# One cross-attention stage on TensorE: values computed once per chunk of keys, in place of context rows summed by the probabilities and projected at the end

## The chip, the cores and the metric

The kernel runs on one NeuronCore of a Trainium2 chip, as one program. Its metric is the time on the device in microseconds. Five engines work side by side, each through its own queue in order: TensorE (PE; its loads of stationary operands are shown as PEld), VectorE (DVE), ScalarE (ACT), GpSimd (POOL) and SyncE (SP), which here issues most of the DMAs. They meet at semaphores alone: every wait in the code is written by hand.

## The reference, cut to what matters

The reference is a small Perceiver block on 128 latent rows of width 256: a cross-attention on a context of 12544 rows (this stage is the one that changes), a banded self-attention, a mixture of experts, a second cross-attention, a scan and a second mixture of experts. The stage in question is

```python
# x1: [1,128,256] (normalised latents), x2: [1,12544,256] (context), 16 heads of 64
q = x1 @ Wq
kv = x2 @ Wkv
k, v = jnp.split(kv, 2, axis=-1)
q, k, v = map(_split_heads, (q, k, v))
attn = jnp.einsum('bhid,bhjd->bhij', q, k) * SCALE
attn = jax.nn.softmax(attn, axis=-1)
out = jnp.einsum('bhij,bhjd->bhid', attn, v)
b, h, l, d = out.shape
out = out.transpose(0, 2, 1, 3).reshape(b, l, h * d)
return out @ Wo + bo
```

All arithmetic is to be that of fp32. The kernel gets there with TensorE's rounded fp32 (F32R): an operand is split into a high part, rounded, and a low part, the rest, and three products (high by high, high by low, low by high) are added in PSUM.

## The kernel before

The stage is `stage_context`. The context is cut into 14 chunks of 896 keys (`CK`; `NT` = 7 tiles of 128). The loop goes over 224 steps, one for each chunk and head: `u = 16 * chunk + head`. Softmax is kept as a running one: `nm` holds the negated maximum, `al` the factor by which the old sums shrink, `den` the denominators, `U` the sums.

Keys are explicit. A "piece" `p` (L494) is half a chunk (448 keys) for a pair of heads, six F32R matmuls into one bank of PSUM; ScalarE writes its high parts (L339) and VectorE its low parts (L405) into the tile `K`. Pieces run five steps ahead (`AHEAD`). The values are not explicit: the probabilities multiply the raw context (`cNh`, `cNl`, 256 wide), `U` holds 256 numbers for each latent and head, and the value weight `wv` comes in after the last step.

One step `u` on TensorE: seven transposes of the probabilities (L553) into two banks, piece `u+5`, the scores of step `u+2` (four matmuls, L504 and L505), and the sum over the keys `O` (L579): 21 matmuls of 256 columns, seven each for high by high, high by low, low by high. ScalarE, meanwhile: high part of the transposed probabilities (`pTh`, L368), high parts of the piece (L339), the factor `al` (L344) and the exponentials of step `u+1` (L346). VectorE: maximum of the scores of step `u+1` (L410) and the new `nm` (L415), low part of the transposed probabilities (`pTl`, L449), low parts of the piece (L405), `den` (L460), and `U = U * al + O` (L463).

After the last step come, for eight pairs of heads, four transposes of `U` (L520), a copy by ScalarE (L353), eight matmuls with `wv` (L533), two copies (L429, L430) and two matmuls with `wo` (L599); two of the pairs are partly done in the last steps. GpSimd splits the context twice a chunk, once as it stands (`cNh`, `cNl`) and once transposed (`cTh`, `cTl`).

Order is set by the code: each engine's instructions stand in the order in which its block writes them. The later stages are the same in both kernels.

## Time and profile before

| | us |
|---|---|
| median of 3 runs (1625.44 to 1628.65) | 1627.57 |
| the profiled execution's own time | 1630.0 |
| its span, first to last instruction | 1628.3 |

| engine | busy us | share of the span |
|---|---|---|
| PE (matmul) | 1541.0 | 95% |
| PEld (weight load, beside PE) | 1448.6 | 89% |
| DVE | 1211.6 | 74% |
| ACT | 910.9 | 56% |
| POOL | 364.7 | 22% |

The mean granted clock of TensorE is 0.973 of full. The steps begin at about 36 us and the last one ends near 1225 us, so some three quarters of the span are this loop; the stage's result is ready at 1243.3 us. Shares are means over stages with different limits; the rows of one step say more. In them the first number is the start, the second the duration, a bracket names how long the engine had been idle and for whom it waited. Matmuls overlap: the distance between two starts, not the duration, is what one costs.

### The profile page before, as it was taken

The numbers are of one execution on the slowest core, as the hardware profiler recorded it, in microseconds if no ns is written. First come the engines' busy times: TensorE is split into PE (matmuls) and PEld (weight loads), VectorE is DVE, ScalarE is ACT, GpSimd is POOL, SyncE is SP. The second block draws the span as 40 slices with busy tenths as digits, with TensorE's granted clock in tenths as the row PEclk, the third lists the DMA queues.
The fourth block names the chain that finished last, engine by engine and source line by source line (L and its number), as shares of the span: only waits on it lengthen the run. The fifth ranks groups of instructions, "written<-read, shape, count | busy, mean of one in ns | idle before, by whom it ended". The sixth has DMA issues, their size and how long they took to land. (4 is left out here: it accounts for less than half of the span.)

```text
span 1628.3 us, 26553 instructions
## 1 busy us (share of the span) xinstructions
PE 1541.0 (95%) x10481; PEld 1448.6 (89%) x10481; DVE 1211.6 (74%) x2060; ACT 910.9 (56%) x1616; POOL 364.7 (22%) x166
## 2 busy tenths in 40 slices
PE   5999999999999999999999999999997889999478
PEld 4999999999999999999999999999995778888348
DVE  5878878878878878878878878888874446666764
ACT  4666666666666666666666666666651245555120
POOL 6211111111111111120303030210000236666230
PEclk8999999999999999999999999999998799999779
DMA  4100000000000001010100000100004412111600
GB/s 149 46 23 24 23 24 24 24 23 24 24 24 23 24 4 43 1 46 1 46 2 26 21 24 24 75 2 1 1 1 168 188 46 68 68 68 45 271 1 4
DMA packets 10321, 70.13 MB, mean 43 GB/s; under 512 B 2313, under 2 KB 2912, under 8 KB 8929
## 3 DMA queue, kind: packets, MB, share of 16 engines
q1 hardware_dynamic: 9198, 67.51, 11.2%
q8 instruction: 77, 1.26, 0.3%
q10 hardware_dynamic: 1010, 1.07, 0.2%
q14 instruction: 36, 0.29, 0.1%
HBM read 68.44 MB, written 0.13 MB: 42 GB/s over the span
## 5 line engine op out<-in xcount | busy, mean ns | idle before, releaser
L368 ACT ACTIVATE pTh<-ps 128x896 fp32r<-128x896 f32 x224 | 206.3, 921 | 352.0 <-PE ps L553 352.0
L405 DVE TENSOR_TENSOR K<-ps,K 64x448 fp32r<-64x448 f32 x448 | 278.8, 622 | 67.4 <-ACT K L339 64.2
L339 ACT CAST K<-ps 64x448 fp32r<-64x448 f32 x448 | 236.9, 529 | 78.2 <-PE ps L494 72.3
L449 DVE TENSOR_TENSOR pTl<-ps,pTh 128x896 fp32r<-128x896 f32 x224 | 244.5, 1092 | 4.0 <-ACT pTh L368 4.0
L410 DVE TENSOR_REDUCE nmx<-ps 128x1 f32<-128x896 f32 x224 | 242.8, 1084 | 2.7 <-PE ps L505 2.7
L346 ACT ACTIVATE prob<-ps,nm 128x896 f32<-128x896 f32 x224 | 226.1, 1009 | 2.7
L579 PEld LDWEIGHTS ps<-cNh,pTh 128*128 128x128 f32 x1568 | 218.0, 190 | 10.0 <-issue 3.0
L579 PE MATMUL ps<-cNh,pTh 128*128 128x256 f32 x1568 | 224.0, 283 | 1.8 <-ACT pTh L368 1.7
L579 PE MATMUL ps<-cNh,pTl 128*128 128x256 f32 x1568 | 225.0, 283 | 0.0
L579 PE MATMUL ps<-cNl,pTh 128*128 128x256 f32 x1568 | 224.7, 283 | 0.0
L463 DVE SCALAR_TENSOR_TENSOR U<-U,al,ps 128x256 f32<-128x256 f32 x224 | 107.5, 480 | 146.3 <-PE ps L579 145.6
L553 PE MATMUL ps<-ident,prob 128*128 128x128 f32 x1568 | 207.8, 273 | 1.5 <-ACT prob L346 1.5
L579 PEld LDWEIGHTS ps<-cNh,pTl 128*128 128x128 f32 x1568 | 204.3, 192 | 0.2
L579 PEld LDWEIGHTS ps<-cNl,pTh 128*128 128x128 f32 x1568 | 204.3, 192 | 0.0
L553 PEld LDWEIGHTS ps<-ident,prob 128*128 128x128 f32 x1568 | 176.8, 142 | 2.1 <-issue 2.1
L270 POOL TENSOR_TENSOR cTh<-raw,zero 128x1792 fp32r<-128x1792 f32 x14 | 44.5, 3176 | 566.4 <-PE ps L494 560.0
L504 PE MATMUL ps<-K,qh 128*128 128x448 f32 x448 | 164.8, 368 | 3.3 <-ACT ql L361 3.3
L505 PE MATMUL ps<-K,ql 128*128 128x448 f32 x448 | 164.5, 367 | 0.0
L494 PE MATMUL ps<-cTh,wkh 128*128 128x448 f32 x448 | 146.6, 408 | 1.4 <-DVE wkh L392 1.4
L494 PE MATMUL ps<-cTh,wkl 128*128 128x448 f32 x448 | 127.7, 366 | 5.2 <-DVE wkl L394 5.2
L494 PE MATMUL ps<-cTl,wkh 128*128 128x448 f32 x448 | 128.8, 368 | 0.0
L270 POOL TENSOR_TENSOR cNh<-raw,zero 128x1792 fp32r<-128x1792 f32 x14 | 44.5, 3175 | 279.9 <-PE ps L579 270.9
(298 smaller groups left out, 2027.3 us busy)
## 6 DMA issues: line engine op xcount, KB each, us to landing
raw<-in_ctxT SPq DMA_DIRECT2D x14, 896.0 KB, 4.6
raw<-in_ctxN SPq DMA_DIRECT2D x14, 896.0 KB, 4.5
d_raw<-in_ctxT SPq DMA_DIRECT2D x14, 896.0 KB, 4.5
w<-in_w SPq DMA_DIRECT2D x2, 4096.0 KB, 18.1
wg<-in_wg SPq DMA_DIRECT2D x1, 4352.0 KB, 25.6
wu<-in_wu SPq DMA_DIRECT2D x1, 4352.0 KB, 18.3
wd<-in_wd SPq DMA_DIRECT2D x1, 4352.0 KB, 28.6
e_ea<-in_alog SPq DMA_DIRECT2D x1, 2048.0 KB, 8.4
```

The costliest lines, as they stand in the source:

```text
L339: nc.scalar.copy(K[halves[s], slot, cols], ps[halves[s], piece_bank(p), 0:HK]).then_inc(sem("kh_ready"), 1)
L346: nc.scalar.activation(prob[:, :, :], S[b], ACT.Exp, bias=nm[:, par, h:h + 1], scale=1.0, accum_out=rs[:, b:b + 1]).then_inc(sem("exp_done ...
L368: nc.scalar.activation(pTh[:, :], pT_ps, ACT.Copy).then_inc(sem("pTh_ready"), 1)
L405: ins = nc.vector.tensor_tensor(K[halves[1 - s], slot, cols], ps[halves[s], piece_bank(p), 0:HK], K[halves[s], slot, cols].bitcast(F32), A ...
L410: nc.vector.tensor_reduce(nmx[:, :], S[u % 2], mybir.AxisListType.XY, ALU.max, negate=True).then_inc(sem("chunk_max"), 1)
L449: nc.vector.tensor_tensor(pTl[:, :], pT_ps, pTh[:, :].bitcast(F32), ALU.subtract).then_inc(sem("pTl_ready"), 1)
L463: nc.vector.scalar_tensor_tensor(U[:, h, :], U[:, h, :], al[:, b:b + 1], O, ALU.mult, ALU.add).then_inc(sem("pv_free"), 1)
L494: mm = nc.tensor.matmul(ps[:, piece_bank(p), 0:HK], w[:, k, m * P:(m + 1) * P], x[:, k, half * HK:(half + 1) * HK], start=(n == 0), stop=( ...
L504: nc.tensor.matmul(S[b][:, half, :], qh[:, h, :], keys, start=True, stop=False)
L505: mm = nc.tensor.matmul(S[b][:, half, :], ql[:, h, :], keys, start=False, stop=True)
L553: mm = nc.tensor.transpose(pT_ps[:, k * P:(k + 1) * P], prob[:, :, :].rearrange("p a n -> p (a n)")[:, k * P:(k + 1) * P], ident[:, :])
L579: mm = nc.tensor.matmul(O, w[:, k * P:(k + 1) * P], x[:, k, :], start=(n == 0), stop=(n == 3 * NT - 1))
```

## The change

The values become explicit, for eight heads (a "group", `HG`) and 896 keys at a time. `values(g, i)` computes 128 keys by 8 heads of 64, six F32R matmuls of 512 columns into bank 6. ScalarE writes the high parts of it and VectorE the low parts, side by side for each head, into one of two tiles `V`. It stands in seven of every eight steps (`v_steps`, 189 in the loop; the first group's seven are computed ahead of it). The sum over the keys then has `V` (high and low, 128 columns) as stationary operand and high and low parts of the probabilities (one tile `pT`, 256 columns) as moving one: 7 matmuls in place of 21, with all four products, transposed (`OT_ps`, in the same bank 6 as the values). VectorE adds the two halves into `osb`, an eighth transpose (`turn_sums`) turns that back, and `U` (now 128 wide: high and low value part) is updated one step later. The end loses its products with `wv`.

Also: the context comes in and is split once, transposed; the raw context `cN` goes. `K` has two pairs of slots (`RING` = 2) in place of three. VectorE computes the maximum two steps ahead in place of one. The wide loads of weights come in halves at the start, the value weight among them; the loads that ScalarE's queue issued are SyncE's now. The diff, cut:

```diff
-        O = ps[:, 6, 0:D]
+        turned = ps[:, 4:6, :].rearrange("p b n -> p (b n)")
+        pT_ps = turned[:, 0:CK].rearrange("p (t q) -> p t q", q=P)
+        O_ps = turned[:, CK:CK + P]
+        OT_ps = ps[:, 6, 0:2 * P]
...
             @block.scalar
...
                 def exp_step(u):
+                    act.wait_ge(sem("max_done"), u + 1)
+                    if u >= 4:
+                        act.wait_ge(sem("u_added"), u - 3)
...
                 for u in range(steps):
                     act.wait_ge(sem("p_turned"), u + 1)
-                    nc.scalar.activation(pTh[:, :], pT_ps, ACT.Copy).then_inc(sem("pTh_ready"), 1)
-                    p = u + AHEAD
-                    if p < steps:
...
-                        high_parts(p)
+                    nc.scalar.activation(pT[:, :, 0, :], pT_ps, ACT.Copy).then_inc(sem("pTh_ready"), 1)
                     if u + 1 < steps:
                         exp_step(u + 1)
+                    if u in v_steps:
+                        j = v_steps.index(u)
+                        act.wait_ge(sem("v_done"), NT + j + 1)
...
+                        nc.scalar.copy(v_high(u // HG + 1, u % HG), by_head(ps[:, 6, :])).then_inc(sem("vh_ready"), 1)
+                    if u + AHEAD < steps:
+                        high_parts(u + AHEAD)
...
             @block.vector
...
+                def add_parts(u):
+                    dve.wait_ge(sem("pv_done"), u + 1)
+                    nc.vector.tensor_reduce(osb[:, :], OT_ps.rearrange("p (a q) -> p q a", a=2), AX_X,
+                                            ALU.add).then_inc(sem("o_added"), 1)
+                def update_sums(u):
+                    h, b = u % H0, u % 4
+                    dve.wait_ge(sem("p_turned"), u + 2)
+                    nc.vector.scalar_tensor_tensor(U[:, h, :], U[:, h, :], al[:, b:b + 1], O_ps,
+                                                   ALU.mult, ALU.add).then_inc(sem("u_added"), 1)
...
                 for u in range(steps):
+                    if u >= 1:
+                        add_parts(u - 1)
+                        if u - 1 + AHEAD < steps:
+                            low_parts(u - 1 + AHEAD)
                     dve.wait_ge(sem("pTh_ready"), u + 1)
+                    nc.vector.tensor_tensor(pT[:, :, 1, :], pT_ps, pT[:, :, 0, :].bitcast(F32),
                                             ALU.subtract).then_inc(sem("pTl_ready"), 1)
+                    if u >= 1:
+                        update_sums(u - 1)
...
                     nc.vector.tensor_scalar(den[:, h:h + 1], den[:, h:h + 1], al[:, b:b + 1],
                                             rs[:, b:b + 1], ALU.mult, ALU.add)
+                    if u in v_steps:
+                        j, g, i = v_steps.index(u), u // HG + 1, u % HG
+                        dve.wait_ge(sem("vh_ready"), j + 1)
+                        nc.vector.tensor_tensor(v_low(g, i), by_head(ps[:, 6, :]), v_high(g, i).bitcast(F32),
+                                                ALU.subtract).then_inc(sem("v_split"), 1)
+                    if u + 2 < steps:
+                        max_step(u + 2)
...
             @block.tensor
...
+                def values(g, i, bank):
+                    c, n = g // 2, 0
+                    cols = (left, right)[g % 2]
+                    for x, w in ((cTh[c % 2], wvh), (cTl[c % 2], wvh), (cTh[c % 2], wvl)):
+                        for k in range(KT):
+                            mm = nc.tensor.matmul(ps[:, bank, :], x[:, k, i * P:(i + 1) * P], w[:, k, cols],
+                                                  start=(n == 0), stop=(n == 3 * KT - 1))
+                            n += 1
+                    mm.then_inc(sem("v_done"), 1)
+                def turn_sums(u):
+                    pe.wait_ge(sem("o_added"), u + 1)
+                    return nc.tensor.transpose(O_ps, osb[:, :], ident[:, :])
...
                 for u in range(steps):
                     pe.wait_ge(sem("exp_done"), u + 1)
...
+                    if u >= 1:
+                        mm = turn_sums(u - 1)
                     mm.then_inc(sem("p_turned"), 1)
-                    p = u + AHEAD
...
                         scores(u + 2)
+                    if u in v_steps:
...
+                        values(gn, i, 6)
+                    p = u + AHEAD
+                    if p < steps:
...
+                        piece(p)
...
+                    pe.wait_ge(sem("pTl_ready"), u + 1)
+                    if u in v_steps:
+                        pe.wait_ge(sem("v_split"), v_steps.index(u) + 1)
...
+                    for k in range(NT):
+                        mm = nc.tensor.matmul(OT_ps, V[g % 2][:, k, h % HG, :],
+                                              pT[:, k, :, :].rearrange("p a q -> p (a q)"),
+                                              start=(k == 0), stop=(k == NT - 1))
                     mm.then_inc(sem("pv_done"), 1)
```

How the order moves is best seen engine by engine. TensorE, one step in the middle of the loop, before (`cN` is the context, `ident` the transposes' identity):

```order
L494 MATMUL ps<-cTh,wkh 128x448 x2
L494 MATMUL ps<-cTh,wkl 128x448 x2
L494 MATMUL ps<-cTl,wkh 128x448 x2
L504 MATMUL ps<-K,qh 128x448
L505 MATMUL ps<-K,ql 128x448
L504 MATMUL ps<-K,qh 128x448
L505 MATMUL ps<-K,ql 128x448
L579 MATMUL ps<-cNh,pTh 128x256 x7
L579 MATMUL ps<-cNl,pTh 128x256 x7
L579 MATMUL ps<-cNh,pTl 128x256 x7
L553 MATMUL ps<-ident,prob 128x128 x7
```

and of the change, from the eighth transpose (L550; the seven before it are L594) to the sum over the keys (L635), lines numbered as in the changed kernel:

```order
L550 MATMUL ps<-ident,osb 128x128
L544 MATMUL ps<-K,qh 128x448
L545 MATMUL ps<-K,ql 128x448
L544 MATMUL ps<-K,qh 128x448
L545 MATMUL ps<-K,ql 128x448
L535 MATMUL ps<-wvh,cTh 128x512 x2
L535 MATMUL ps<-wvh,cTl 128x512 x2
L535 MATMUL ps<-wvl,cTh 128x512 x2
L524 MATMUL ps<-cTh,wkh 128x448 x2
L524 MATMUL ps<-cTh,wkl 128x448 x2
L524 MATMUL ps<-cTl,wkh 128x448 x2
L635 MATMUL ps<-pT,V 128x256 x7
```

The scores stand ahead of the piece now, the values between them, and 14 of the 21 wide matmuls are gone. VectorE over the same step, before:

```order
L410 TENSOR_REDUCE nmx<-ps 128x1
L415 TENSOR_SCALAR nm<-nmx,nm 128x1
L449 TENSOR_TENSOR pTl<-ps,pTh 128x896
L405 TENSOR_TENSOR K<-ps,K 64x448 x2
L460 TENSOR_SCALAR den<-den,al,rs 128x1
L463 SCALAR_TENSOR_TENSOR U<-U,al,ps 128x256
```

and of the change (`osb` is the sum of the halves, `V` the low parts of the values):

```order
L438 TENSOR_REDUCE osb<-ps 128x128
L422 TENSOR_TENSOR K<-ps,K 64x448 x2
L480 TENSOR_TENSOR pT<-ps,pT 128x7x128
L444 SCALAR_TENSOR_TENSOR U<-U,al,ps 128x128
L486 TENSOR_SCALAR den<-den,al,rs 128x1
L491 TENSOR_TENSOR V<-ps,V 128x8x64
L430 TENSOR_REDUCE nmx<-ps 128x1
L433 TENSOR_SCALAR nm<-nmx,nm 128x1
```

The maximum has moved from the head of the step to its end, behind the low parts of the values and ahead of the next sum of halves. ScalarE, one step and the head of the next, in the change (before, the casts of `K` stood right behind the copy of the transposed probabilities, and there was no `V`):

```order
L381 ACTIVATE pT<-ps 128x7x128
L361 ACTIVATE al<-nm 128x1
L363 ACTIVATE prob,rs<-ps,nm 128x896
L392 CAST V<-ps 128x8x64
L353 CAST K<-ps 64x448 x2
L381 ACTIVATE pT<-ps 128x7x128
```

The high parts of the values come behind the exponentials of the next step.

## Rows read from the trace of the kernel before

**Rows 1.** Busy time by window: PE, PEld, DVE, ACT, POOL, clock, DMA, GB/s
```profile
60.00:1220.00 1160.00, 1158.32 (x8294) 1124.24 (x8293) 937.37 (x1545) 733.92 (x1306) 173.69 (x48) 1.00 0.06 21
1215.00:1226.00 11.00, 9.09 (x72) 8.21 (x72) 6.81 (x16) 3.71 (x6) 0.00 (x0) 1.00 0.00 0
1243.00:1262.00 19.00, 12.94 (x38) 8.68 (x38) 11.45 (x29) 0.41 (x2) 1.80 (x2) 0.73 0.89 359
```

**Rows 2.** Timeline of one step, weight loads: start us, us, engine, line
```profile
605.51 0.30 PEld L494 LDWEIGHTS ps<-cTh,wkh 128*128 128x128 f32 x2
...
606.63 0.19 PEld L504 LDWEIGHTS ps<-K,qh 128*128 128x128 f32 x1
...
607.44 0.99 PEld L579 LDWEIGHTS ps<-cNh,pTh 128*128 128x128 f32 x7
...
610.06 0.79 PEld L553 LDWEIGHTS ps<-ident,prob 128*128 128x128 f32 x7
```

**Rows 3.** The same step, ScalarE
```profile
605.82 0.92 ACT L368 ACTIVATE pTh<-ps 128x896 fp32r<-128x896 f32 x1 [1.58 <-PE ps L553]
607.03 1.08 ACT L339 CAST K<-ps 64x448 fp32r<-64x448 f32 x2 [0.30 <-PE ps L494]
608.14 0.29 ACT L344 ACTIVATE al<-nm 128x1 f32<-128x1 f32 x1
608.45 1.01 ACT L346 ACTIVATE prob<-ps,nm 128x896 f32<-128x896 f32 x1
609.36 0.19 ACT L346 ACTIVATION_READ_ACCUMULATOR prob<-ps,nm 128x1 f32 x1
```

**Rows 4.** The same step, VectorE
```profile
605.45 1.08 DVE L410 TENSOR_REDUCE nmx<-ps 128x1 f32<-128x896 f32 x1
606.57 0.21 DVE L415 TENSOR_SCALAR nm<-nmx,nm 128x1 f32<-128x1 f32 x1
606.77 1.09 DVE L449 TENSOR_TENSOR pTl<-ps,pTh 128x896 fp32r<-128x896 f32 x1
608.15 1.26 DVE L405 TENSOR_TENSOR K<-ps,K 64x448 fp32r<-64x448 f32 x2 [0.29 <-ACT K L339]
609.44 0.27 DVE L460 TENSOR_SCALAR den<-den,al,rs 128x1 f32<-128x1 f32 x1
610.36 0.48 DVE L463 SCALAR_TENSOR_TENSOR U<-U,al,ps 128x256 f32<-128x256 f32 x1 [0.65 <-PE ps L579]
```

**Rows 5.** The same step, the last two matmuls of the piece
```profile
606.43 0.57 PE L494 MATMUL ps<-cTl,wkh 128*128 128x448 f32 x2
```

**Rows 6.** Groups by form, 512-wide casts and subtractions of the later cross-attention
```profile
L1160 DVE TENSOR_TENSOR d_kNl<-ps,d_kNh 128x512 fp32r<-128x512 f32 x42 | 27.4, 681 | 1.1 <-ACT d_kNh L1095 1.1
L1095 ACT CAST d_kNh<-ps 128x512 fp32r<-128x512 f32 x42 | 23.5, 597 | 28.4 <-PE ps L1238 28.4
```

**Rows 7.** Timeline near the loop's end, where TensorE waits for VectorE
```profile
1217.64 0.21 DVE L415 TENSOR_SCALAR nm<-nmx,nm 128x1 f32<-128x1 f32 x1
1217.77 1.08 DVE L449 TENSOR_TENSOR pTl<-ps,pTh 128x896 fp32r<-128x896 f32 x1
...
1218.91 0.90 PEld L579 LDWEIGHTS ps<-cNh,pTl 128*128 128x128 f32 x7
...
1220.05 0.48 DVE L463 SCALAR_TENSOR_TENSOR U<-U,al,ps 128x256 f32<-128x256 f32 x1 [1.01 <-PE ps L579]
```

**Rows 8.** Timeline around the first step, a matmul at the low clock and the first copy
```profile
32.37 0.57 PE L504 MATMUL ps<-K,qh 128*128 128x448 f32 x1
...
37.27 0.92 ACT L368 ACTIVATE pTh<-ps 128x896 fp32r<-128x896 f32 x1 [1.14 <-PE ps L553]
```

**Rows 9.** Timeline of the stage's end: last copy of probabilities, last projection, result
```profile
1221.25 0.92 ACT L368 ACTIVATE pTh<-ps 128x896 fp32r<-128x896 f32 x1 [0.18 <-PE ps L553]
...
1242.17 0.70 PE L599 MATMUL ps<-wo,oT 128*128 128x256 f32 x2 [0.67 <-DVE oT L430]
1242.91 0.42 DVE L472 TENSOR_TENSOR res<-res,ps 128x256 f32<-128x256 f32 x1 [0.79 <-PE ps L599]
```

More of the change, by code:

```diff
@@ L468, in _ @@
+                    if u + 2 < steps:
+                        max_step(u + 2)
+                    m = (u - (steps - H0)) // 2 - 1
+                    if u > steps - H0 and u % 2 == 0:
+                        scale_sums(m)
+                add_parts(steps - 1)
+                update_sums(steps - 1)
                 scale_sums(PAIRS - 1)
-                for m in range(EARLY, PAIRS):
-                    outputs(m)
                 dve.wait_ge(sem("y0_done"), 1)
@@ new lines, in turn_heads, with project @@
+                def turn_heads(pairs, bank):
+                    pe.wait_ge(sem("U_scaled"), pairs[-1] + 1)
+                    for i, m in enumerate(pairs):
+                        mm = nc.tensor.transpose(ps[:, bank, i * P:(i + 1) * P], U[:, 2 * m, :], ident[:, :])
+                    mm.then_inc(sem("heads_turned"), 1)
+                def project(pairs):
+                    for m in pairs:
+                        mm = nc.tensor.matmul(ps[:, 0, 0:D], oT[:, m, :], wo[:, m, :], start=False,
+                                              stop=(m == PAIRS - 1))
+                    return mm
@@ new lines, in _ @@
+                pe.wait_ge(sem("cT_split"), 1)
+                pe.wait_ge(sem("wk_split"), 1)
+                piece(0)
+                piece(1)
+                piece(2)
+                piece(3)
+                pe.wait_ge(sem("kl_ready"), 1)
+                piece(4)
+                pe.wait_ge(sem("wv_split"), 1)
+                for i in range(NT):
+                    if i == 2:
+                        pe.wait_ge(sem("ql_doubled"), 2)
+                        pe.wait_ge(sem("kl_ready"), 2)
+                        scores(0)
+                        scores(1)
+                    if i < 3:
+                        pe.wait_ge(sem("kl_ready"), i + 2)
+                    else:
+                        pe.wait_ge(sem("first_vl"), i - 1)
+                    values(0, i, first_bank(i))
@@ L604, in stage_mix1 @@
+                project((7,)).then_inc(sem("y0_done"), 1)
 def stage_mix1(nc, t, sb, sem, link, ps, norms, v):
@@ L1701, in layout @@
         "x": a["x"][0],
-        "ctxN": ctx.reshape(n, NT, P, D).transpose(0, 2, 1, 3),
         "ctxT": ctx.reshape(n, CK, KT, P).transpose(0, 3, 2, 1),
```

397 lines of the change are left out of this document (176 added, 221 removed).

## The prediction

> **What bounds the kernel now.** I read the table of windows first. Over the loop [rows 1] the matmuls are busy 1158.3 of 1160 us at the full granted clock, VectorE 81% and ScalarE 63%. A share alone proves nothing, so I went on to the timeline of one step. TensorE's weight loads follow each other without a gap [rows 2]: piece from 605.51 to 606.63 (1.12 us for six matmuls), scores to 607.44 (0.81 for four, 0.20 each), the 21 matmuls of the sum to 610.06 (2.62, 0.125 each), transposes 0.76 (0.11 each). That is 5.31 us, the whole step. ScalarE and VectorE wait for it: 1.58 us ahead of the copy of the probabilities [rows 3], 0.65 us ahead of the update of U [rows 4]. So TensorE's own load is the bound, and taking work from it pays only until some chain of waits takes over.
>
> **TensorE's load after.** A step with values: eight transposes 0.87, scores 0.81, six matmuls of 512 columns 1.37 (0.20 x 512/448 = 0.229 each, an estimate) [rows 2], piece 1.12, sum over the keys 7 x 0.125 = 0.87; together 5.04 us. A step without them: 3.67. Over 189 and 34 steps (the 223 between the first copy and the last) that is 1077 us, where now 1184.0 lie between these copies [rows 8, 9]: 107 us less.
>
> **VectorE's and ScalarE's load after.** VectorE keeps low parts of the piece 1.26, pTl 1.09, den 0.27, maximum 1.08 and nm 0.21 [rows 4]; the update of U falls from 0.48 to about 0.35, as 128 elements fewer at the rate between the 256 of that row and the 896 of pTl, which is 0.95 ns each. It gains the low parts of the values, 0.68 [rows 6], and the sum of halves. For that no row stands: it reads 256 elements from PSUM, and from the maximum's 1.08 for 896 at the same rate it is 0.48 at most and not below 0.40. I take 0.42. By the Trainium skill, "VectorE: DVE Perf Modes", section on the TRN2 errata, a PSUM source costs 120 cycles and one per element at 0.96 GHz, which would be an estimate of 0.39 and 7 us less in all; the rows here run dearer than that rule, 1.08 us for 896 elements where it gives 1.06. The sum on VectorE is 5.4 us, about 4.9 when the 0.08 by which an instruction starts ahead of the end of the one before (1217.77 against 1217.85) [rows 7] is taken off six times. ScalarE: 0.92, 1.41, 0.60 and 1.08, about 4.1. No engine's load reaches the old 5.31 us. The chain does.
>
> **The ring.** Three waits close it: TensorE may not sum over the keys in step u until VectorE has split this same step's values (both live in bank 6); ScalarE takes those values only behind the exponentials; and the copy of the next probabilities waits for the eighth transpose, that is for VectorE's sum of halves, ahead of which VectorE now runs the maximum. I walk it from the start of ScalarE's copy in step u, with 0.03 for a hand-over from ScalarE (606.74 to 606.77) [rows 3, 4] and 0.06 from VectorE to TensorE (1218.85 to 1218.91) [rows 7].
> - Copy 0.92, then al, exponentials and accumulator: 608.14 to 609.55 is 1.41 [rows 3]. ScalarE is free at 2.36.
> - Are the values there? The eighth transpose's load is at -0.42 (it is 0.42 ahead of the copy: the copy starts 0.31 after the next load of TensorE, and one transpose is 0.11) [rows 2, 3]. Scores end at 0.50, the last load of the values is 5 x 0.229 later, and the result is readable 0.60 after the last load (606.43 to 607.03) [rows 3, 5] plus 0.03 for the wider matmul: 2.28. So ScalarE's order decides, by only 0.1 us.
> - High parts of the values: 2.39 to 2.99, 0.60 [rows 6]. Low parts: 3.02 to 3.70.
> - TensorE starts the sum at 3.76; VectorE could read it 1.14 later (1218.91 to 1220.05) [rows 7], at 4.90. VectorE, meanwhile, runs maximum and nm: start 3.62, nm 1.12 later (605.45 to 606.57) [rows 4], next start 0.13 later [rows 7], 4.87. The two are level.
> - Sum of halves 4.88 to 5.30, eighth transpose's load at 5.36, next copy 0.42 later: **5.78 us** for a step with values.
>
> TensorE idles 0.7 us of it, from the end of the piece's loads (0.50 + 1.37 + 1.12 = 2.99) to 3.76. The low parts of keys fit between the sum of halves and the arrival of the high parts of probabilities (they would end at 0.74, pTl starts at 0.95). The high parts of keys run on ScalarE from 3.0 to 4.1 behind the values, with 1.7 us to spare; that cover hides them.
>
> A step without values: copy 0.92, pTl 0.95 to 2.04, sum over the keys from 2.10, readable at 3.24. VectorE has by then update of U, den and the maximum to do (from 1.96: 0.27, 0.20, 1.12, 0.13), free at 3.68; sum of halves to 4.09, load at 4.15, next copy 4.57.
>
> **The sum.** Loop: 189 x 5.78 + 34 x 4.57 = 1092.4 + 155.4 = 1247.8 us, against 1184.0: +63.8. That TensorE does 107 us less and the loop still takes longer is the whole point: the new order buys load with latency.
>
> The end: now 22.1 us from the last copy to the result (1221.25 to 1243.33) [rows 9]. After: copy and pTl 2.04, sum over keys readable at 3.24, halves 3.66, turned 4.14, U 4.49, scaling (three small instructions, about 0.25 each) 5.2, one transpose 5.65, one copy of about 0.4 6.05, projection readable 0.74 later [rows 9] 6.8, addition 0.42: 7.2. That is 14.9 us less; the other pairs lie under the last steps, where TensorE has room.
>
> The start: the first copy is at 37.27 now [rows 8]. Seven blocks of values (9.6 us of TensorE, 4.8 of VectorE) come in ahead of step 0, the first of them under keys' evacuation, and VectorE's long split of the key weight is cut in halves. A walk of it came out within 2 us of the present; I take 0, with -6 to +10 as bounds. The input DMAs are not near any limit in the loop (6% busy) [rows 1], one of the two context transfers goes and GpSimd does half its splits: nothing there waits or is waited for. The later stages are the same: 0.
>
> Sum: +63.8 - 14.9 = +49 us. On the profiled execution's span that is 1677, with the 1.7 around it 1679; on the median 1627.57 it is 1676.5. I forecast **1676 us**.
>
> **Rivals.**
> 1. TensorE's load stays the bound (faster). The ring would have to be shorter than its 5.04 us, for instance since hand-overs, the accumulator's readout or the maximum cost less in it than I add. Time: 1628 - 107 - 15 = 1506. The point from which the sign turns is a value step of 5.78 - 49/189 = 5.52; between it and 5.04 the time lies between. For it: three of my links are level within 0.1 us, so none has hidden slack that adds. Against it: eleven links from rows would have to be 0.26 too long together, and they repeat here within 0.01 from step to step. Chance 0.12, most of it just under 1628.
> 2. TensorE's clock falls (slower). It now pauses some 0.7 us in each value step. At the low level a matmul of 448 columns takes 0.57 in place of 0.37 [rows 8], so 0.20 more for each of four scores, 0.23 for each of six values, 0.1 for each of seven in the sum: about 3 us more in a step. If the clock is low in a tenth of the loop, that is +60: 1736. Against it: between 1215 and 1226 matmuls were busy 9.09 of 11 us, with pauses of a microsecond, at clock 1.00; it fell to 0.73 only where they were busy 12.9 of 19 us [rows 1]. After the change they are busy about seven eighths. Chance 0.07. By the Trainium skill, "TensorE: Matmul & The Clock Gate", section on psum-queue depth-cycling, small idles between groups of matmuls through PSUM can make the clock oscillate; by that rule rival 2 would be the rule and not the exception, and the window of 1215 to 1226 disagrees with it.
> 3. A strided read of PSUM costs twice (slower). The sum of halves steps 128 elements between its two addends. At 0.69 in place of 0.42 it is on the ring every step: 223 x 0.27 = +60, 1737. No row has that pattern. Chance 0.06.
>
> **How the numbers follow.** The forecast holds 0.72: its own range is a ring of 5.6 to 5.95 us (+-34), halves 0.40 to 0.48 (-4 to +13), start -6 to +10, in all 1636 to 1722. A tie with before, 1624 to 1631, gets 0.03 (0.2% either way is what a measurement here can tell from no change). Faster is rival 1, 0.12; slower the rest, 0.85. The range for 8 in 10: 1632 to 1728.
>
> **What would show it.** In the profile after: value steps of 5.8 us and every eighth of 4.6; ScalarE going from the accumulator's readout to the cast of V with almost no wait; TensorE waiting for V of VectorE ahead of the sum over the keys, 0.6 to 0.8 us, 189 times; the maximum ending within 0.1 us of the sum over the keys; granted clock 1.00 in the loop; the stage's end about 7 us after the last copy. I am wrong if TensorE's loads run without a gap (rival 1), if the clock in the loop is below 0.97 (rival 2), if the sum of halves takes over 0.5 us (rival 3), or if ScalarE idles ahead of the cast of V by more than 0.2 us, since then the values come late and the ring goes through TensorE.

## The result and the profile after

The change makes the kernel slower: the median is 1656.68 us (4 runs, 1656.43 to 1657.95) against 1628.11 us (4 runs) for the kernel before on the same chip. The ratio is 1.0175, with a 95% interval of 1.0152 to 1.0197. The forecast was 1676 us in a range of 1632 to 1728, with a chance of 0.85 for slower. The direction is as forecast, clear of the noise but under 2%; of the 49 us forecast, 28.6 came.

| | before | after | |
|---|---|---|---|
| span, us | 1628.3 | 1654.7 | +26.4 |
| start of the first copy of probabilities | 37.27 | 41.49 | +4.2 |
| from the first to the last of these copies | 1184.0 | 1221.5 | +37.5 |
| from the last copy to the stage's result | 22.1 | 9.5 | -12.6 |
| the later stages | 385.0 | 382.2 | -2.8 |

(The rows of before for the first three lines are those of [rows 8, 9].) First the page's line of busy times in the profile after, then its windows (length, then PE, PEld, DVE, ACT, POOL, clock, DMA, GB/s), the first over the loop as [rows 1] was, the second at the stage's end.

```profile
PE 1510.1 (91%) x8657; PEld 1285.2 (78%) x8657; DVE 1368.0 (83%) x2467; ACT 970.2 (59%) x1807; POOL 247.3 (15%) x141
```

```profile
60.00:1240.00 1180.00, 1122.75 (x6490) 959.39 (x6489) 1074.89 (x1919) 784.53 (x1477) 68.93 (x24) 1.00 0.03 10
1262.00:1272.00 10.00, 9.40 (x35) 6.55 (x33) 2.95 (x8) 1.66 (x3) 0.00 (x0) 0.73 0.00 0
```

TensorE's loads fell from 97% of the loop to 81%, and VectorE's share rose from 81% to 91%: no engine is full any more, at a granted clock of 1.00 throughout. That is what a ring looks like in shares. The timeline of one value step of the profile after, TensorE's loads (start us, us, engine, line), without the piece and most of the scores and values:

```profile
602.04 0.14 PEld L550 LDWEIGHTS ps<-ident,osb 128*128 128x128 f32 x1
602.13 0.19 PEld L544 LDWEIGHTS ps<-K,qh 128*128 128x128 f32 x1
602.24 0.19 PEld L545 LDWEIGHTS ps<-K,ql 128*128 128x128 f32 x1
...
606.09 0.89 PEld L635 LDWEIGHTS ps<-pT,V 128*128 128x128 f32 x7 [0.62 <-issue]
...
607.69 0.14 PEld L550 LDWEIGHTS ps<-ident,osb 128*128 128x128 f32 x1
```

ScalarE and VectorE in the same step:

```profile
602.44 0.92 ACT L381 ACTIVATE pT<-ps 128x896 fp32r<-128x896 f32 x1 [1.12 <-PE ps L550]
603.25 0.28 ACT L361 ACTIVATE al<-nm 128x1 f32<-128x1 f32 x1
603.44 1.00 ACT L363 ACTIVATE prob<-ps,nm 128x896 f32<-128x896 f32 x1
604.33 0.19 ACT L363 ACTIVATION_READ_ACCUMULATOR prob<-ps,nm 128x1 f32 x1
604.66 0.59 ACT L392 CAST V<-ps 128x512 fp32r<-128x512 f32 x1
...
608.09 0.92 ACT L381 ACTIVATE pT<-ps 128x896 fp32r<-128x896 f32 x1 [1.12 <-PE ps L550]
...
605.28 0.69 DVE L491 TENSOR_TENSOR V<-ps,V 128x512 fp32r<-128x512 f32 x1 [0.35 <-ACT V L392]
605.88 1.08 DVE L430 TENSOR_REDUCE nmx<-ps 128x1 f32<-128x896 f32 x1
607.00 0.21 DVE L433 TENSOR_SCALAR nm<-nmx,nm 128x1 f32<-128x1 f32 x1
607.21 0.42 DVE L438 TENSOR_REDUCE osb<-ps 128x128 f32<-128x256 f32 x1
```

Read around the ring (the closed chain of waits that the prediction walked), from one load of the eighth transpose to the next: 602.04 to the cast of V at 604.66 is 2.62; to the low parts at 605.28, 0.62; to the load of the sum over the keys at 606.09, 0.81; to the sum of halves at 607.21, 1.12; to the next load at 607.69, 0.48. That is 5.65 us. Steps without values take 4.48. (These are the most frequent distances. In the last chunk every second step is longer, 6.12 and 5.07, of which more below.) The waits of the whole execution (engine, line, for whom: us in all, times, longest) show the same ring from outside:

```profile
ACT pT L381 <- PE ps L550: 253.5, 223, 3.0
PEld ps L635 <- issue: 115.4, 189, 0.6
DVE V L491 <- ACT V L392: 65.7, 189, 0.7
```

Three waits come once in every value step (the first in the others too): for the eighth transpose 1.1 us, for V 0.35 us, and TensorE's 0.6 us ahead of the sum over the keys, 189 times.

### The profile page after: what moved, and what is told of

Same layout as the page of the kernel before. It is cut to its first block and busy times, and to the rows that moved or that the text cites. A ratio compares the mean times of both kernels' runs of the same rounds, so it can differ in the third digit from the quotient of the medians.

```text
span 1654.7 us, 23818 instructions
## 1 busy us (share of the span) xinstructions
PE 1510.1 (91%) x8657; PEld 1285.2 (78%) x8657; DVE 1368.0 (83%) x2467; ACT 970.2 (59%) x1807; POOL 247.3 (15%) x141
## 5 line engine op out<-in xcount | busy, mean ns | idle before, releaser
L381 ACT ACTIVATE pT<-ps 128x896 fp32r<-128x896 f32 x224 | 206.1, 920 | 253.6 <-PE ps L550 253.5
L635 PEld LDWEIGHTS ps<-pT,V 128*128 128x128 f32 x1568 | 199.5, 188 | 125.6 <-issue 115.4
L635 PE MATMUL ps<-pT,V 128*128 128x256 f32 x1568 | 236.4, 290 | 54.9 <-DVE V L491 42.9
L480 DVE TENSOR_TENSOR pT<-ps,pT 128x896 fp32r<-128x896 f32 x224 | 244.5, 1092 | 30.4 <-ACT pT L381 6.8
L594 PE MATMUL ps<-ident,prob 128*128 128x128 f32 x1568 | 208.2, 273 | 0.0
L491 DVE TENSOR_TENSOR V<-ps,V 128x512 fp32r<-128x512 f32 x189 | 130.7, 691 | 65.7 <-ACT V L392 65.7
L594 PEld LDWEIGHTS ps<-ident,prob 128*128 128x128 f32 x1568 | 177.2, 141 | 0.1
L535 PE MATMUL ps<-wvh,cTh 128*128 128x512 f32 x392 | 123.6, 397 | 4.0 <-DVE V L468 4.0
L392 ACT CAST V<-ps 128x512 fp32r<-128x512 f32 x189 | 110.9, 587 | 23.4 <-PE ps L535 0.2
L535 PE MATMUL ps<-wvl,cTh 128*128 128x512 f32 x392 | 123.3, 396 | 0.0
L535 PE MATMUL ps<-wvh,cTl 128*128 128x512 f32 x392 | 122.7, 394 | 0.0
L524 PEld LDWEIGHTS ps<-cTh,wkh 128*128 128x128 f32 x448 | 81.6, 188 | 35.1 <-DVE K L422 17.7
```

Of the source, the lines that this page charges most:

```text
L381: nc.scalar.activation(pT[:, :, 0, :], pT_ps, ACT.Copy).then_inc(sem("pTh_ready"), 1)
L480: nc.vector.tensor_tensor(pT[:, :, 1, :], pT_ps, pT[:, :, 0, :].bitcast(F32), ALU.subtract).then_inc(sem("pTl_ready"), 1)
L524: mm = nc.tensor.matmul(ps[:, piece_bank(p), 0:HK], w[:, k, m * P:(m + 1) * P], x[:, k, half * HK:(half + 1) * HK], start=(n == 0), stop=( ...
L535: mm = nc.tensor.matmul(ps[:, bank, :], x[:, k, i * P:(i + 1) * P], w[:, k, cols], start=(n == 0), stop=(n == 3 * KT - 1))
L594: mm = nc.tensor.transpose(pT_ps[:, k, :], prob[:, :, :].rearrange("p a n -> p (a n)")[:, k * P:(k + 1) * P], ident[:, :])
L635: mm = nc.tensor.matmul(OT_ps, V[g % 2][:, k, h % HG, :], pT[:, k, :, :].rearrange("p a q -> p (a q)"), start=(k == 0), stop=(k == NT - 1))
```

## The experiments

Where an interval stands, the kernel was timed in rounds beside the kernel before; the others are single executions. "Step" is the most frequent distance between two copies of the probabilities in the profile, for steps with values and without. Unless said otherwise, diffs are against the changed kernel.

### The same step with TensorE's order turned

Two blocks change places, one after the other. First, on TensorE, the values ahead of the scores:

```diff
                     mm.then_inc(sem("p_turned"), 1)
-                    if u + 2 < steps:
-                        ...
-                        scores(u + 2)
                     if u in v_steps:
                         ...
                         values(gn, i, 6)
+                    if u + 2 < steps:
+                        ...
+                        scores(u + 2)
```

> The changed kernel with one move on TensorE: the six matmuls of the values stand ahead of the scores, not behind them. Theory (the ring through bank 6: eighth transpose, scores, values, cast of V, low parts of V, sum over the keys, sum of halves): in the changed kernel ScalarE waits 0.14 us for the values ahead of the cast of V (604.52 to 604.66), and back to back it would start 0.10 ahead of the end of its accumulator readout, so the cast comes 0.24 us earlier and then hangs on ScalarE's own order: value step 5.65 to 5.41, span about 1610. Rival 1 (TensorE's load is the bound, as before): its load is the same, so 5.65 stays, 1655. Rival 2 (VectorE's load is the bound): 5.65 stays as well, 1655.

Measured: 1613.24 us, ratio 0.9903 (0.9879 to 0.9928); steps of 5.41 and 4.48. Its timeline of a value step, ScalarE and TensorE's loads:

```profile
600.95 0.20 ACT L363 ACTIVATION_READ_ACCUMULATOR prob<-ps,nm 128x1 f32 x1
601.04 0.58 ACT L392 CAST V<-ps 128x512 fp32r<-128x512 f32 x1
...
602.46 0.89 PEld L635 LDWEIGHTS ps<-pT,V 128*128 128x128 f32 x7 [0.38 <-issue]
```

No TensorE work was saved, only moved, and the step falls by 0.24. The cast now starts 0.09 after the accumulator's readout started, that is before it ends: ScalarE's queue has become what is late, and the values no longer are. So in the changed kernel the values' arrival was on the ring, and ScalarE's own order stood only 0.24 behind it.

Then, besides, the cast of V ahead of the exponentials on ScalarE:

```diff
                     nc.scalar.activation(pT[:, :, 0, :], pT_ps, ACT.Copy).then_inc(sem("pTh_ready"), 1)
-                    if u + 1 < steps:
-                        exp_step(u + 1)
                     if u in v_steps:
                         ...
                         nc.scalar.copy(v_high(u // HG + 1, u % HG), ...).then_inc(sem("vh_ready"), 1)
+                    if u + 1 < steps:
+                        exp_step(u + 1)
```

> As v1, and ScalarE casts V ahead of the exponentials of the next step, not behind them. Theory of the ring: the values are readable 1.81 us after the eighth transpose's load, cast done at 2.40, VectorE gets to the low parts when pTl, the update of U and den are done (2.80 after that load), sum over the keys from 3.61, readable 4.73, halves, load of the next eighth transpose at 5.21. Value step 5.21 (TensorE's own load is 5.12, from the trace of the changed kernel), span about 1572, under the kernel before. Rival 1 (TensorE's load is the bound already): no change to 5.65. Rival 3 (the exponentials, now later, come too late for the next transposes, which only trades one wait for another): they would be ready 3.6 us after the eighth transpose's load and are needed at 4.5; if a hand-over is longer than it looks, TensorE waits for ScalarE ahead of the transposes and the step stays near 5.6.

Measured: 1577.53 us, ratio 0.968 (0.9657 to 0.9704); steps of 5.20 and 4.48. Its timeline, VectorE from one sum of halves to the next, and TensorE's one wait:

```profile
600.45 0.42 DVE L438 TENSOR_REDUCE osb<-ps 128x128 f32<-128x256 f32 x1
...
603.54 0.27 DVE L486 TENSOR_SCALAR den<-den,al,rs 128x1 f32<-128x1 f32 x1
603.72 0.68 DVE L491 TENSOR_TENSOR V<-ps,V 128x512 fp32r<-128x512 f32 x1
...
605.65 0.42 DVE L438 TENSOR_REDUCE osb<-ps 128x128 f32<-128x256 f32 x1
...
604.52 0.89 PEld L635 LDWEIGHTS ps<-pT,V 128*128 128x128 f32 x7 [0.17 <-issue]
```

VectorE never waits for V now (603.72 follows 603.54 directly): 600.45 to 605.65 is 5.20 us of its own instructions, but for a tenth ahead of the low parts of the probabilities, which start 0.03 behind the end of ScalarE's copy (601.33 + 0.92, against 602.28). The arithmetic is that of the changed kernel, instruction for instruction, and 79 us are gone. The loss was in the order of two queues.

### Which resource the step feels

More TensorE work in each piece from the sixth on (two more matmuls of 448 columns, overwritten by the next):

```diff
+                    if p >= AHEAD:
+                        for _ in range(2):
+                            nc.tensor.matmul(ps[:, piece_bank(p), 0:HK], wkh[:, 0, m * P:(m + 1) * P],
+                                             cTh[c % 2][:, 0, half * HK:(half + 1) * HK], start=True, stop=True)
```

> The changed kernel with two more matmuls ahead of each piece of keys in the loop (the piece's first product, computed three times, the first two overwritten): 0.41 us more of TensorE's load in each step and nothing else. Theory of the ring: TensorE stands still for 0.62 us ahead of the sum over the keys in a value step, so this is hidden: value step 5.65, non-value steps up to 0.3 longer, span 1655 to 1665. Rival 1 (TensorE's load is the bound): +0.41 in 219 steps, about 1745.

Measured: 1666.29 us, steps of 5.67 and 4.56. Some 0.4 us of load came into every step and the value step took 0.02 of it. In the others TensorE's wait behind the piece is for the sum of halves and is shorter, 0.35 (a row of the run without values, below); they took 0.08. In a value step TensorE's wait shrank instead, from 0.62 to this:

```profile
604.55 0.89 PEld L639 LDWEIGHTS ps<-pT,V 128*128 128x128 f32 x7 [0.21 <-issue]
```

The sum of TensorE's work doesn't bound the value step.

Half of the cast of V (from the third group on ScalarE writes only four of the eight heads' high parts, 256 columns of 512):

```diff
-                        nc.scalar.copy(v_high(u // HG + 1, u % HG), by_head(ps[:, 6, :])).then_inc(...)
+                        ...
+                            nc.scalar.copy(V[(u // HG + 1) % 2][:, u % HG, 0:4, 0:DH0],
+                                           by_head(ps[:, 6, 0:4 * DH0])).then_inc(sem("vh_ready"), 1)
```

> The changed kernel, in which ScalarE casts only the first 256 of the 512 columns of V from the second group of eight heads on (the high parts of four heads in eight are left stale). A cast of 256 columns took 0.39 us where one of 512 took 0.59. Theory of the ring: the cast is on it with its full length and VectorE waits 0.35 us for it, so 182 value steps lose 0.20 each: 5.65 to 5.45, span about 1619. Rivals 1 and 2 (load of TensorE or of VectorE): neither loses anything, 1655.

Measured: 1617.52 us, steps of 5.43 and 4.48. ScalarE and VectorE in its timeline:

```profile
604.38 0.37 ACT L395 CAST V<-ps 128x256 fp32r<-128x256 f32 x1
...
604.78 0.69 DVE L495 TENSOR_TENSOR V<-ps,V 128x512 fp32r<-128x512 f32 x1
```

The cast fell by 0.22 (0.59 to 0.37) and the value step by 0.22: ScalarE idles a third of the loop, but this one instruction of it counts in full.

Half of the maximum (over the first 224 of each 448 keys; the exponentials are shifted by that value then):

```diff
-                    nc.vector.tensor_reduce(nmx[:, :], S[u % 2], mybir.AxisListType.XY, ALU.max,
+                    nc.vector.tensor_reduce(nmx[:, :], S[u % 2][:, :, 0:HK // 2], mybir.AxisListType.XY, ALU.max,
```

> The changed kernel with the maximum taken over half of each chunk's keys only (448 of 896 scores, the other half left out): 0.47 us less on VectorE in every step. Theory: in a value step the sum over the keys is readable at the moment VectorE is free (607.18 against 607.21), so there it gives 0.03 to 0.06; in the other steps VectorE decides and 0.44 go; 189 x 0.05 + 34 x 0.44 = 24, span about 1630. Rival 2 (VectorE's load is the bound of the changed kernel): 0.47 in all 223 steps, 1550.

Measured: 1637.88 us, steps of 5.65 and 4.12. VectorE does 0.47 less in each step, and this is where it goes in a value step:

```profile
603.04 0.42 DVE L438 TENSOR_REDUCE osb<-ps 128x128 f32<-128x256 f32 x1 [0.46 <-PE ps L635]
```

It waits for the sum over the keys instead; only steps without values gain, 0.36 each. So VectorE's maximum did not bound a value step: the sum over the keys came as late or later.

Values for the first two groups alone (182 of the 189 blocks of values, with their casts and low parts, left out; later steps use the values of those groups; two waits that follow from it are changed too):

```diff
-    v_steps = [u for u in range(steps - HG) if u % HG < NT]
+    v_steps = [u for u in range(HG) if u % HG < NT]
```

> The changed kernel with the values computed for the first two groups alone; all later groups use stale ones (182 of 189 blocks of values left out, matmuls, casts and low parts). Theory: every step is then one without values, 4.48 us: 182 x 1.17 = 213 us less, span about 1442; the block of values costs the loop 1.17 us where TensorE spends 1.40 on it. Rival 1 (TensorE's load, 3.7 us without values): the steps fall to 3.7, span near 1300.

Measured: 1452.22 us, steps of 4.48 from the second group on. TensorE waits twice for VectorE in each, which leaves it a load of 3.6 us:

```profile
604.41 0.14 PEld L550 LDWEIGHTS ps<-ident,osb 128*128 128x128 f32 x1 [0.35 <-DVE osb L438]
...
605.70 0.30 PEld L524 LDWEIGHTS ps<-cTh,wkh 128*128 128x128 f32 x2 [0.52 <-DVE K L422]
```

Without any value work the step is VectorE's: 4.48 us, so a value costs the step 5.65 - 4.48 = 1.17 us. The total came 10 us above the expectation, although the step came out exactly. Four of them are the start: the first copy was at 45.5 us in this execution, against 41.5 in the changed kernel's. The loop was 5 us longer than expected, 1.5 of it in its last step but one (6.06 against 4.54) and some 3 since the value steps that went were 5.64 as a mean and not 5.65. The other 1 us or so is in what the single executions differ by.

### How much the kernel before had to give

The kernel before with its product of high probabilities by low context left out (14 wide matmuls per step in place of 21):

```diff
-                    for w, x in ((pTh, cNh[c % 2]), (pTh, cNl[c % 2]), (pTl, cNh[c % 2])):
-                        if n == 2 * NT:
+                    for w, x in ((pTh, cNh[c % 2]), (pTl, cNh[c % 2])):
+                        if n == NT:
```

> The kernel before with one of its three products in the sum over the keys left out (high probabilities by low context): 14 matmuls for 21, 0.84 us less on TensorE in every step. Reading of the kernel before (TensorE's load is its bound): step 5.31 to about 4.47, span about 1442, as VectorE's load there is 4.4 us. Rival (a chain just below TensorE's load already decides): the step stays above 4.8.

Measured: 1518.28 us, a step of 4.81 where I expected 4.47. It misses by 76 us, and the rival reading beside it held: a chain stands just below TensorE's load. Its timeline:

```profile
603.08 1.01 ACT L346 ACTIVATE prob<-ps,nm 128x896 f32<-128x896 f32 x1
...
604.23 0.74 PEld L553 LDWEIGHTS ps<-ident,prob 128*128 128x128 f32 x7 [0.32 <-ACT prob L346]
```

TensorE waits for the exponentials, which stand behind the casts of K, which wait for the piece. With that old order the step can lose 0.5 us of load (5.31 to 4.81), whatever TensorE saves beyond it. So rival 1's 107 us of saved load were not all to be had with the old order. If the same floor of 4.81 held with values in the step (an estimate from these rows; no run tested it), a value step could give its 0.27 (5.31 to 5.04) and the others 0.50 in place of 1.64: 189 x 0.27 + 34 x 0.50 = 68 us.

### Towards a faster version

With both orders turned, VectorE pauses once, 0.1 us ahead of the low parts of the probabilities. The update of `den` goes into that pause (diff against the second kernel above):

```diff
+                    dve.wait_ge(sem("exp_done"), u + 1)
+                    ...
+                    nc.vector.tensor_scalar(den[:, h:h + 1], den[:, h:h + 1], al[:, b:b + 1], ...)
                     dve.wait_ge(sem("pTh_ready"), u + 1)
...
-                    nc.vector.tensor_scalar(den[:, h:h + 1], den[:, h:h + 1], al[:, b:b + 1], ...)
```

> v2 with the update of den on VectorE moved ahead of pTl. Theory: in v2 VectorE has no gap left but 0.1 us ahead of pTl, so its own load (5.20) is the bound; den fills that gap, the chain behind pTl is 0.12 shorter and TensorE's load of 5.11 is met: value step 5.11, the others 0.1 shorter, span about 1558. Rival (the chain copy, pTl, low parts, maximum is not what ends last): 5.20 stays, 1578.

Measured: 1584.22 us, steps of 5.23 and 4.51: a miss, 0.03 slower a step where 0.09 faster was expected. VectorE in its timeline:

```profile
606.54 0.27 DVE L482 TENSOR_SCALAR den<-den,al,rs 128x1 f32<-128x1 f32 x1
606.83 1.09 DVE L485 TENSOR_TENSOR pT<-ps,pT 128x896 fp32r<-128x896 f32 x1
```

From `den` to the next start are 0.29 us here; where it stood before, between U and V, they were 0.18 (603.54 to 603.72). The pause was a real one, but a small one: from the start of the low parts of K it is 1.29 us to a `den` right behind them (605.25 to 606.54) and was 1.37 to the low parts of the probabilities (600.91 to 602.28), which waited for ScalarE's copy. So `den` filled 0.08 and cost 0.11 more than in its old place: 0.03 longer, as measured.

The next kernel has that order too, and repairs both ends: scores of steps 0 and 1 ahead of the first values, and the projection of four pairs behind the last sum over the keys.

```diff
-                    if i == 2:
+                    if i == 0:
                         pe.wait_ge(sem("ql_doubled"), 2)
...
-                        pe.wait_ge(sem("oT_ready"), 1)
-                        project(range(0, 4))
...
                         turn_heads((4, 5, 6), 7)
+                        pe.wait_ge(sem("oT_ready"), 1)
+                        project(range(0, 4))
```

> v2 (values ahead of the scores on TensorE, cast of V ahead of the exponentials on ScalarE) with three more moves: VectorE updates den ahead of pTl, where it waits a moment for ScalarE's copy; the scores of steps 0 and 1 come ahead of the first values (ScalarE had stood still 5.5 us at the start for them); the projection of the first four pairs comes behind the last sum over the keys, which it had held up by 2 us. Theory: the loop goes with v3, to 5.11 a step, the start comes 2 to 3 us earlier and the end 2 us: span about 1554, clearly under the kernel before. Rival: the start and the end are bound by something else (VectorE's low parts at the start, the slow clock at the end), then 1558.

Measured: 1579.18 us, ratio 0.9677 (0.9658 to 0.9696); steps of 5.23 and 4.51. Another miss, by 25 us: the step is that of the kernel above, and the end did not get shorter (11.1 us from the last copy to the result, 10.3 in the second kernel). The window ahead of it, and TensorE behind the last sum:

```profile
1172.00:1188.00 16.00, 10.82 (x57) 9.22 (x56) 9.39 (x22) 6.58 (x14) 0.00 (x0) 0.81 0.00 1
```

```profile
1192.15 3.61 PE L561 MATMUL ps<-wo,oT 128*128 128x256 f32 x8
...
1195.57 0.31 PE L551 MATMUL ps<-ident,osb 128*128 128x128 f32 x1
```

The projection is ahead of the last eighth transpose now instead of ahead of the last sum: it holds up the same chain one link later. It is slow as well: the granted clock was 0.55 from 1192 to 1196 us. The start did improve: its first copy is at 39.25 us.

That part alone, on the second kernel:

```diff
-                    if i == 2:
+                    if i == 0:
                         pe.wait_ge(sem("ql_doubled"), 2)
```

> v2 with the scores of steps 0 and 1 ahead of the first values only. Theory: ScalarE's fifth piece waits for these scores (two pairs of slots in K), 5.5 us in the changed kernel; v4 had its first copy 5.3 us ahead of v3's. The loop stays at 5.20: span about 1573. Rival: the start is bound by the DMAs or by VectorE, and it stays at 1578.

Measured: 1574.37 us, ratio 0.9656 (0.9628 to 0.9684); steps as in the second kernel, the first copy at 39.65 where it was 43.41.

Last, VectorE's load itself goes down. `den` moves to GpSimd, where the splits of the context are issued between its updates, and the low parts of V stand right behind those of the probabilities (diff against the kernel just above):

```diff
+                for u in range(steps):
+                    ...
+                    pool.wait_ge(sem("exp_done"), u + 1)
+                    ...
+                    nc.gpsimd.tensor_scalar(den[:, h:h + 1], den[:, h:h + 1], al[:, b:b + 1],
+                                            rs[:, b:b + 1], ALU.mult, ALU.add).then_inc(sem("den_added"), 1)
...
-                    if u >= 1:
-                        update_sums(u - 1)
-                    ...
-                    nc.vector.tensor_scalar(den[:, h:h + 1], den[:, h:h + 1], al[:, b:b + 1], ...)
                     if u in v_steps:
                         ...
+                    if u >= 1:
+                        update_sums(u - 1)
```

> v2 with the scores of steps 0 and 1 ahead of the first values, with den updated on GpSimd (which reads al and rs from SBUF) and with VectorE's low parts of V right behind pTl. Theory (in v2 and v3 VectorE has no gap left, its load of 5.20 and 5.23 is the bound; v3 only moved den to a place where it cost 0.29 in place of 0.18): without den VectorE needs 5.02 in a value step and TensorE's 5.11 is the bound; the other steps go from 4.48 to 4.30; loop 23 us shorter than v2's, start 5 shorter, span about 1550. Rival (GpSimd's den comes so late behind its splits that ScalarE waits for it ahead of al, or slows VectorE through SBUF): steps near a split get longer, and v6 is no better than v5.

Measured: 1560.31 us, ratio 0.9572 (0.9545 to 0.9598), the fastest of all; steps of 5.15 and 4.30. Its timeline, TensorE's loads of one step, then VectorE, then GpSimd in an earlier step:

```profile
620.18 0.14 PEld L555 LDWEIGHTS ps<-ident,osb 128*128 128x128 f32 x1
...
623.21 0.40 PEld L529 LDWEIGHTS ps<-cTl,wkh 128*128 128x128 f32 x2
623.62 0.98 PEld L640 LDWEIGHTS ps<-pT,V 128*128 128x128 f32 x7
624.55 0.79 PEld L599 LDWEIGHTS ps<-ident,prob 128*128 128x128 f32 x7
625.33 0.14 PEld L555 LDWEIGHTS ps<-ident,osb 128*128 128x128 f32 x1
...
622.59 0.69 DVE L494 TENSOR_TENSOR V<-ps,V 128x512 fp32r<-128x512 f32 x1
...
624.85 0.42 DVE L446 TENSOR_REDUCE osb<-ps 128x128 f32<-128x256 f32 x1
...
608.41 0.34 POOL L343 TENSOR_SCALAR den<-den,al,rs 128x1 f32<-128x1 f32 x1 [5.04 <-ACT prob L371]
```

V's low parts end at 623.28 and TensorE asks for them at 623.62, behind its own loads without a gap: the value step is TensorE's load again, as it was before the change, only shorter (620.18 to 625.33, 5.15, against 5.31). VectorE's sum of halves is level with it: it ends at 625.27, 0.06 ahead of the load that needs it. The expectation was missed by 10 us, most of it since it put this load at 5.11. The change pays once two queues are reordered around it, and more with VectorE's made shorter; the loop is 59 us under that of the kernel before (1124.8 against 1184.0).

## Why the prediction was right, and where its sizes were off

**What bounded the kernel, and the direction: right.** TensorE's load fell by about what was counted (a value step holds 5.03 us of it, 5.65 less the wait of 0.62; 5.04 was forecast; without any wait it is 5.15, in the last kernel, where the piece stands behind matmuls of 448 columns and takes 1.23 and not 1.12, and the sum over the keys 0.93 and not 0.87), the loop took longer all the same, and the added matmuls of the filler kernel, all but free in a value step, show that load was no longer the bound.

**The ring: right in kind, 0.13 too long in each value step.** This is the step that was mis-sized. Forecast 5.78 and measured 5.65; 189 x 0.13 = 25 us, and 34 x 0.09 = 3 us for the others. Some 4 us of that went again in the last chunk, below, and the loop came 26.3 us under the forecast. The other terms by the profiles: the start 4.2 us above the forecast, the end 2.3 above, the later stages 2.8 below. Together that is 22.6 us; by the medians the miss is 20. Link by link, from the load of the eighth transpose:

| link | forecast | after |
|---|---|---|
| to the cast of V | 2.81 | 2.62 |
| to the low parts of V | 0.63 | 0.62 |
| to the load of the sum over the keys | 0.74 | 0.81 |
| to the sum of halves | 1.12 | 1.12 |
| to the next load of the eighth transpose | 0.48 | 0.48 |
| sum | 5.78 | 5.65 |

The first link rested on "ScalarE's order decides, by only 0.1 us". It does not. I had put 0.03 after the copy and taken the exponentials' 1.41 from a place where they followed a cast [rows 3]; in the new order ScalarE is free 2.08 us after the copy's start, not 2.36. So ScalarE waits 0.14 us for the values, and 0.24 counted from the start that it could have had (1.98 after the copy, in the first reordered kernel). The distances behind it: `al` 0.81 after the copy and not 0.95, `prob` 0.19 after `al` and not 0.31, the readout 0.89 after `prob` and not 0.91. The values also came some 0.08 earlier than forecast: the first of the scores' loads is followed by the next after 0.11 and not 0.20 (602.13 to 602.24); here the matmul ahead is a transpose of 128 columns and not one of 448. I had taken the scores' stretch from a place behind the piece [rows 2]. The list of what would make me wrong had this case, with more than 0.2 us of idle time ahead of the cast. The recorded 0.14 is under that bound, and the reading named there holds all the same: the kernel with values ahead of scores gained 0.24 by it.

**The hand-over to TensorE: too short.** 0.12 us from the end of V's low parts (605.97) to the load, where 0.06 had been read from one wait near the loop's end [rows 7]. Some 11 us in all (189 x 0.06), which hid part of the first miss.

**Level chains: right, and the most useful line of the walk.** The maximum and the sum over the keys were forecast to end within 0.03 of each other. Halving the maximum gained nothing that can be read in value steps (5.65 both times): the sum over the keys ended last. By how much shows where nothing holds VectorE: there 0.13 pass from `nm` to the sum of halves, here 0.21 (607.00 to 607.21), so it was 0.08.

**The sum of halves: right.** 0.42 each time, taken 0.42. Rival 3 (a strided read costs twice) falls. The estimate of 0.39 by the Trainium skill, "VectorE: DVE Perf Modes", section on the TRN2 errata, would have been 0.03 short.

**The steps without values: 4.57 forecast, 4.48 measured**, VectorE's chain as said; 0.05 of the difference is the copy's distance to a lone transpose (0.37, not 0.42), the rest is hundredths in U and `den`.

**The last chunk: put at nothing.** There VectorE scales the finished sums of a pair of heads in every second step, and in the new order these three instructions stand between the maximum and the sum of halves, on the ring:

```profile
1242.14 0.21 DVE L433 TENSOR_SCALAR nm<-nmx,nm 128x1 f32<-128x1 f32 x1
1242.27 0.15 DVE L450 RECIPROCAL rden<-den 128x2 f32<-128x2 f32 x1
...
1242.64 0.29 DVE L453 TENSOR_TENSOR U<-U,rden 128x128 f32<-128x128 f32 x1
1242.85 0.42 DVE L438 TENSOR_REDUCE osb<-ps 128x128 f32<-128x256 f32 x1
```

From `nm` to the sum of halves that is 0.71 in place of 0.13 to 0.21. Such steps take 6.12 us with values and 5.07 without, three of each, and the last step, part of it at the low clock, 5.24: some 4 us. In the kernel before, such scaling stood in steps that kept their 5.31, under TensorE's load.

**The start: wrong by 4 us.** Forecast 0 (bounds -6 to +10), measured +4.2 in this pair of executions. With two pairs of slots for K, the cast of the fifth piece waits for the scores of step 1, which stood behind two blocks of values; in the profile after ScalarE stood still for 5.53 us:

```profile
28.99 1.08 ACT L353 CAST K<-ps 64x448 fp32r<-64x448 f32 x2 [5.53 <-PE ps L545]
```

The kernel with the scores first gained 3.8 us at its first copy. With the same code at the start, single executions had it at 41.5 to 45.5 us, so the size is rough.

**The end: 7.2 forecast, 9.5 measured.** TensorE, around the last step, then VectorE:

```profile
1264.06 3.58 PE L560 MATMUL ps<-wo,oT 128*128 128x256 f32 x8
1267.28 1.18 PE L635 MATMUL ps<-pT,V 128*128 128x256 f32 x7
...
1272.12 0.42 DVE L502 TENSOR_TENSOR res<-res,ps 128x256 f32<-128x256 f32 x1 [1.71 <-PE ps L560]
```

I had taken four pairs' projection as lying under the last steps. It is issued ahead of the last sum over the keys and takes 3.2 us up to 1267.21, where the low parts of the probabilities had been ready since 1265.06: 2.1 us of the 2.3 that the end came out too long. About half of those 3.2 us is the clock, which was 0.50 of full from 1262 to 1267.2 us: the six matmuls of 1269.36, back at full clock, take 1.16 us of loads, 0.19 each, the eight of 1264.06 3.06, 0.38 each.

**The later stages: 2.8 us less**, forecast 0. Their code is the same. No run here explains it; it is about the spread between executions of one kernel and stays open.

**The rivals.** Rival 1 (TensorE's load stays the bound) did not come; the last kernel's orders bring it about. Its point of 5.52 for the sign was near: with start, end and later stages as measured the gain begins at 5.51, and the half-cast kernel at 5.43 and the first reordering at 5.41 lie just on the other side (1617.5 and 1613.2 us). Rival 2 (the clock) falls for the loop: 1.00 over 1180 us with 0.6 us of pause in every value step. The Trainium skill, "TensorE: Matmul & The Clock Gate", section on psum-queue depth-cycling, tells of a kernel whose clock oscillates through short, frequent idle times of this kind, without their length. By that rule the clock would have oscillated here; this trace disagrees. Behind the last steps the clock did fall, which is the projection's slow stretch above.

## What to carry to other kernels

When a change removes load from the bounding engine and adds a producer, a splitter and a consumer within one step, walk the ring before counting the load, and let the walk choose the order: what the ring waits for goes to the head of each queue, what only has to be done by the next step goes behind it. Here that order alone turned 1656.7 us into 1577.5. And read a link's duration from the same pair of neighbours as it will have: the misses of the ring came mostly from distances read beside other neighbours. Walk the loop's first and last steps too: small work that lay under the bounding engine's load may stand on the ring now.

## What the runs showed of the hardware

- ScalarE starts an instruction 0.1 us ahead of the end of the one before when nothing holds it: copy of 0.92, next start 0.81 later; readout of the accumulator of 0.20, cast 0.09 after its start.
- The price of a small instruction on VectorE depends on its neighbours: `den` (0.27) costs 0.18 between the update of U and V's low parts, and 0.29 between the low parts of K and those of the probabilities. It costs 0.29 too between the low parts of K and the update of U, in the kernel before with 14 wide matmuls; whether the neighbour ahead or the one behind decides was not separated.
- The same instruction on GpSimd takes 0.34 us and was hidden 224 times, 77 us in all; that engine's share is 21% with them, and 15% in the changed kernel without.
- Where TensorE's loads follow each other without a gap, the distance from one load to the next is that of the matmul ahead of both: 0.11 us behind a transpose of 128 columns, 0.20 behind 448, 0.23 behind 512.
- TensorE's granted clock stayed at 1.00 with pauses of 0.6 us in steps of 5.65. In the last steps of the kernel with both ends changed it was 0.81 as a mean of its two levels (1.2 and 2.4 GHz), with matmuls busy 10.82 of 16 us; in the changed kernel it was 1.00 from 1240 to 1260 us, with matmuls busy 12.29 of these 20 us, 0.50 from 1262 to 1267.2, and 1.00 again from 1270.
